# Layer 1's fronts in a two-layer mixer and expert kernel: both turned halves in one step, the row maximum a step behind the logits, scatters laid evenly and ended two steps ahead of the routed jobs

## The reference: what is computed

```python
x = L0_attn_x                                  # (4, 1024, 128)
xn = _layernorm(x)
s = _L0_attn_ref(xn, ...)   # a state-space scan over time, 256 channels x 16 states
g = _silu(_L0_ffn_ref(xn, ...))   # 8 experts, top 2, and a shared expert
x = x + s * g
xn = _layernorm(x)
s = _L1_attn_ref(xn, ...)   # linear attention, no softmax
g = _silu(_L1_ffn_ref(xn, ...))   # 8 experts of hidden size 176, top 2, and a gated shared one
x = x + s * g
```

## Time and profile before

| | |
|---|---|
| three runs | 1098.51, 1099.65, 1100.06 us; median 1099.65 us |
| the profiled execution, its own time | 1098.78 us |
| its span, first to last instruction | 1096.6 us |
| DVE busy | 940.8 us (86% of the span) |
| PE busy | 813.8 us (74%), mean granted clock 0.906 |
| POOL busy | 618.6 us (56%) |
| ACT busy | 577.2 us (53%) |
| scan of step 143, the last, begins | at 1028.97 us |
| from there to the end of the span | 67.6 us |

### The profile page before, as it was taken

One profiled execution on the slowest core, in us unless ns is written; L12 is line 12 of the kernel. 1 busy time (PEld: TensorE's weight loads), 2 busy tenths in 40 slices (PEclk: granted clock), 3 DMA queues, 4 the chain that ended last, 5 costly groups with the idle time before them and its releaser, 6 DMA issues.

```text
span 1096.6 us, 15959 instructions
## 1 busy us (share of the span) xinstructions
PE 813.8 (74%) x4378; PEld 595.6 (54%) x4378; DVE 940.8 (86%) x1608; ACT 577.2 (53%) x1296; POOL 618.6 (56%) x421
## 2 busy tenths in 40 slices
PE   7557576877877778768787678776686767678786
PEld 3444464565655656556665556564464645566564
DVE  5999989889988888999989979997979978879565
ACT  4446353665657455745566455645454535445333
POOL 1435885323678337534754776684885737623670
PEclk9778696999999989989999999998987889989998
DMA  8955954333444356435644447345753346446301
GB/s 250 266 162 151 250 145 129 111 90 90 128 120 140 94 140 168 129 80 141 171 109 119 128 139 183 95 146 152 180 140 79 101 112 185 112 93 137 99 27 34
DMA packets 169060, 146.07 MB, mean 133 GB/s; under 512 B 14433, under 2 KB 135825, under 8 KB 168977
## 3 DMA queue, kind: packets, MB, share of 16 engines
q10 hardware_dynamic: 38960, 66.00, 24.6%
q1 hardware_dynamic: 122337, 63.31, 20.2%
q0 software_dynamic: 7680, 15.74, 4.7%
HBM read 106.59 MB, written 37.88 MB: 132 GB/s over the span
## 4 chain that ended last, share of the span: by engine, by line
DVE 40%; PE 24%; issue 14%; POOL 7%; DMA 6%; ACT 6%; SPq 1%; ACTq 1%; DVEq 0%; POOLq 0%
DVE pA L1621 15%; DVE hj L1656 4%; POOL dBx L875 4%; PE pR L1125 3%; PE pGU L1084 3%; DVE hc L1629 3%; POOL rows_in L816 3%; PE pH L1010 3%; PE pGU L1081 3%; PE pGU L1082 3%; DMA xg<-rows_in 3%; DVE ca L1403 3%; DVE hj L1668 2%; ACT hT L1350 1%; DMA rows_in<-xn,slots 1%
## 5 line engine op out<-in xcount | busy, mean ns | idle before, releaser
L875 POOL TENSOR_TENSOR dBx<-dtx,bcb 128x1024 f32<-128x1024 f32 (+1 forms) x143 | 302.3, 2114 | 354.5 <-DVE pA L1621 323.0
L1010 PE MATMUL pH<-const,hc 128*128 128x128 f32 x1024 | 157.9, 301 | 100.7 <-DVE hc L1629 82.7
L1010 PEld LDWEIGHTS pH<-const,hc 128*128 128x128 f32 x1024 | 128.3, 155 | 122.8 <-DVE hc L1629 101.8
L1147 ACT ACTIVATE pA<-dt,am 128x512 f32<-128x512 f32 (+1 forms) x286 | 172.5, 637 | 27.9 <-DVE hc L1629 20.3
L1621 DVE TENSOR_TENSOR_SCAN pA<-pA,carry,dBx 128x512 f32<-128x512 f32 (+1 forms) x160 | 162.7, 1062 | 9.6 <-POOL dBx L875 5.5
L1629 DVE TENSOR_TENSOR hc<-pA,bcb 128x1024 f32<-128x1024 f32 (+1 forms) x144 | 159.3, 1106 | 5.0
L1621 DVE TENSOR_TENSOR_SCAN pA<-pA,dBx 128x512 f32<-128x512 f32 x128 | 149.7, 1215 | 4.5 <-ACT pA L1147 2.8
L1656 DVE SCALAR_TENSOR_TENSOR hj<-tj,pGU 128x352 f32<-128x352 f32 (+2 forms) x181 | 87.3, 482 | 59.0 <-ACT tj L1333 19.5
L834 POOL DMA_INDIRECT gy<-rows_out,slots x96 | 99.8, 1039 | 24.5 <-issue 19.9
L1099 PE MATMUL pR<-const,hj 128*88 128x128 f32 (+2 forms) x594 | 104.2, 291 | 9.4 <-issue 2.3
L1350 ACT ACTIVATE hT<-pR 128x384 f32<-128x384 f32 (+2 forms) x186 | 95.3, 512 | 13.9 <-PE pR L1099 12.5
(11 more groups left out here) (247 smaller groups left out, 1450.4 us busy)
## 6 DMA issues: line engine op xcount, KB each, us to landing
bcb<-bc_rows ACTq DMA_DIRECT2D x109, 512.0 KB, 5.0
xg<-rows_in SPq DMA_DIRECT2D x162, 64.0 KB, 2.8
bcb<-bc_rows ACTq DMA_DIRECT2D x32, 256.0 KB, 5.0
rows_out<-yj SPq DMA_DIRECT2D x114, 64.0 KB, 2.5
rows_out<-yj SPq DMA_DIRECT2D x54, 128.0 KB, 3.1
rows_in<-gy SPq DMA_DIRECT2D x12, 512.0 KB, 10.4
mixed<-s_st SPq DMA_DIRECT2D x12, 256.0 KB, 2.5
so<-rows_out SPq DMA_DIRECT2D x6, 512.0 KB, 4.7
```

The costliest lines, as they stand in the source:

```text
L875: pool.tensor_tensor(dBx[:, N % 2, :, 0:t1 - t0], dtx[q % 2][:, :, t0:t1], row, ALU.mult).then_inc(dBx_ready, 1)
L1010: last = mm(pH[:, half, c * DI + k * P:c * DI + (k + 1) * P], hc[:, N % 2, k, t * P:(t + 1) * P], ident, is_transpose=True, start=(n == 0 ...
L1147: A(pA[:, k, 0:t1 - t0], dt[q % 2][:, k, t0:t1], ACT.Exp, scale=am[:, k, n:n + 1]).then_inc(decay_ready, 1)
```

## The change

Only the table of `make_plan` changes; no instruction's shape does, and the computation stays the same.

```diff
-FFN3_AT, GATHER1_AT, GATHER2_AT = 107, 118, 139
+FFN3_AT, GATHER1_AT, GATHER2_AT = 107, 117, 135
...
-    FRONT = dict(first=1, norm=2, xn=3, xT=4, logits=6, top=7, route=8, pick=9, rank=10, slots=11, experts=14, scatter=12)
+    FRONT = dict(first=1, norm=2, xn=3, xT=4, logits=5, top=6, route=7, pick=8, rank=9, slots=10, experts=13, scatter=11)

-    def scatters(l, j, s, per_step):
+    def scatters(l, j, s, over):
         count = TOPK * cols(l, j)[1]
         for i in range(count):
-            at(s + i // per_step, "scatter", l, j, i)
-        return s + 1 + count // per_step
+            at(s + i * over // count, "scatter", l, j, i)
+        return s + over + (l == 1)
-
-    def front(b, s, per_step=3, **moved):
+    def front(b, s, over=5, **moved):
...
-            at(o["xT"] + 1, "xT", 1, b, 1)
+            at(o["xT"], "xT", 1, b, 1)
...
-        avail[1, b, "shared"] = o["xT"] + (2 if whole else 1)
-        avail[1, b, "routed"] = max(scatters(1, b, o["scatter"], per_step), o["experts"] + 1)
+        avail[1, b, "shared"] = o["xT"] + 1
+        avail[1, b, "routed"] = max(scatters(1, b, o["scatter"], over), o["experts"] + 1)
...
-    front(2, 96, 4, first=3, norm=3, xn=4, xT=6, logits=9, top=9, route=10, pick=11, rank=12, slots=13, experts=14, scatter=14)
+    front(2, 96, 4, first=3, norm=3, xn=4, xT=5, logits=6, top=7, route=8, pick=9, rank=10, slots=11, experts=13, scatter=12)
...
-    front(LAST, 7 * NS, 2, first=2, norm=2, xn=3, xT=5, logits=6, top=6, route=7, pick=8, rank=9, slots=10, experts=12, scatter=11)
-    front(LAST + 1, 8 * NS, first=1, norm=1, xn=2, xT=3, logits=4, top=4, route=5, pick=6)
+    front(LAST, 7 * NS, 3, first=2, norm=2, xn=3, xT=4, logits=5, top=6, route=7, pick=8, rank=9, slots=10, experts=12, scatter=11)
+    front(LAST + 1, 8 * NS, first=1, norm=1, xn=2, xT=3, logits=4, top=5, route=6, pick=6)
...
         for i in range(TOPK * CT):
-            at(s1 + i // (3 if b else 4), "gather", 1, b, i)
-        for part, step in zip(range(-1, 7), ((104, 106, 107, 108, 111, 113, 115, 116), (121, 124, 125, 126, 127, 129, 131, 132),
+            step = (s1 + i // 4, s1 + (i // 2 if i < 10 else 8 + (i - 10) // 3), s1 + i if s1 + i < STEPS else STEPS + 1)[b]
+            at(step, "gather", 1, b, i)
+        for part, step in zip(range(-1, 7), ((104, 106, 107, 108, 111, 113, 115, 116), (121, 127, 128, 129, 130, 132, 133, 134),
```

More of the change, by code:

```diff
@@ L187, in make_plan @@
         at(experts_at, "experts", 0, g)
-        avail[0, g, "routed"] = scatters(0, g, s + 5, 3)
+        avail[0, g, "routed"] = scatters(0, g, s + 5, 11)
     at(61, "x3T")
```

## The result

The changed kernel took **1115.8 us** (median of four executions, 1113.17 to 1128.33) against 1099.9 of the kernel before: a ratio of 1.015, 95% interval 1.0109 to 1.0191. It is slower; I had forecast 1095. In three of four later series of timings, each on another chip, the same kernel stood at 1.0018 (0.9991 to 1.0046), 1.0017 (0.9988 to 1.0047) and 1.0101 (1.0062 to 1.014) of before. So the loss lies between 1 and 16 us by the series: clear in the first comparison and the last, not to be told from zero in the two between, and a gain in none. The ratios leave out one execution of the kernel before that took 2178.8 us.

The account below looks back on a forecast made before the run. DVE, the busiest engine, was taken to bound the kernel, so terms counted idle time given back or taken; they summed to a gain of 4.5 us from the profiled 1098.78: 1094.3, or 1095 by the median. Range 1085 to 1102.

Parts of the forecast that it names:

- The fronts of batches 0 and 1: Steps 81 and 97: routed tiles a step earlier mostly move the waits; gain 1.8 and loss 1.0 us.
- The row maximum: Row maximum a step behind the logits: waits of 5.3 us in step 105 and 2.3 in step 132 go; gain 7.6.
- My rival of no change: Step 105's 5.3 us was ACT's queue, and the gate behind may wait for it instead: 1100 or 1098 us; chance 0.20.
- Batch 2, -0.55 net: Steps 108 to 115: wait of 6.2 us goes, POOL's load costs 5.7, gain 0.5; step 114's new gate loses 1.05.
- `dBx` as the releaser in steps 109 to 112: Sign that the forecast was right: DVE waits there for `dBx` on overloaded POOL, taken as 5.2 us over the stretch.
- Batch 1's fetch, -4.3: Steps 116 to 120: tiles behind the earlier fetch reach step 119's gate late; 30.8 against 26.47 us, loss 4.3.
- The wait at job 151's gate: Sign in step 119: 8 to 10 us if the forecast was right, under 4 if wrong.
- Way back of batch 1, -1.3: Steps 121 to 128: more indirect DMAs on POOL make DVE wait 9.7 to 11 us; loss 1.3.
- 22.4 to 24 us: Time from the start of step 123 until POOL issues the last gather of step 126.
- Gathers one a step, +3.9: Steps 135 to 142: batch 2's gathers one a step, 3.45 us a step, 27.6 + 0.3 against 31.79; gain 3.9.
- Behind the scans, -1.7: After the last scan's start: 15 gathers instead of 9 on POOL delay `combine`, one dense slot less; loss 1.7 us.

Follow-up runs that it names:

- second pair: Second profiles of the unaltered changed kernel (1106.69 us) and of the unaltered kernel before (1102.82 us), taken in two later series on two chips.
- second column: Stretch-by-stretch difference, changed kernel less kernel before, between the second profiles of each, from two later series on two chips: sum +4.7 us.

## Why the prediction was wrong, step by step

**The step that failed.** I added up idle gaps of DVE and gave each back, and put at nothing what the same entries do on POOL. Two terms show it. The fronts of batches 0 and 1, forecast as +0.8, alone made the kernel 3.7 us slower: steps 83 to 96, for which I had no term, took 5.5 more, in DVE instructions held by POOL. The row maximum was to give 5.3 in step 105 and gave 0.7. A third step had no term either: batch 2's fetch went from step 139 to 135, one step behind batch 1's store, and steps 135 to 142, forecast at -3.9, took 0.7 more (1.3 less in the second pair).

- **Row maximum, +7.6: failed in method.** In step 105 I gave the whole wait of 5.3 back and did not ask who is ready next. It was POOL, with 7.28 us a step and 0.75 idle; 0.7 came back. My rival of no change had this form, but named ACT. For the 2.3 of step 132, steps 129 to 134 were 1.1 shorter than in the first profile of before and 3.4 shorter than in the second.
- **Batches 0 and 1, +0.8: wrong by 5.5 us.** The gates of steps 81 and 97 waited 4.35 and 6.61, as worked out, and steps 64 to 82 gained 2.1. What I left out is steps 83 to 96. I had costed POOL's load in steps 108 to 112 and not in 91 to 95, where the same evenly laid scatters meet the same kind of addition (4.6 us in step 92), nor asked what POOL does during the wait that I moved out of step 82 (2.6 us in step 83). With the scatters back, both were gone.
- **Batch 2, -0.55 net: right that POOL is overloaded, wrong in the sign.** I had named `dBx` as the releaser in steps 109 to 112. DVE never waited for it there; it met the load as held instructions, 4.7 us of it in `cmp` and 1.3 to 1.4 in each of two operations on `w13a`. Steps 108 to 112 took 40.4 and 38.7 us for a forecast of 36.8; over 108 to 115 the size was off by 3.1 in the first profile and 1.7 in the second. The 3.35 us that I took for POOL's addition, here and behind the scans, was a held one; alone it takes 2.36.
- **Batch 1's fetch, -4.3: right.** 31.57 us for a forecast of 30.8; with the fetch moved back 27.4. Over all profiles it is 30.7 to 31.9 in six with the fetch in 117, and 26.0 to 28.2 in nine with it in 118, 30.0 in a tenth. The wait at job 151's gate was 4.4, not 8 to 10: the gate came 23.4 us into step 116 and not 25, and DVE had already waited 2.6 us in smaller pieces. What the term rests on is the measured way, 20.1 us from store to gate. That the tiles "cannot overtake" the fetch was more than the Trainium skill, "DMA: Bandwidth & Descriptors", section "Queues, rings and completion order", states: by it descriptors are taken in ring order, but DMAs need not complete in the order of their issue.
- **Way back of batch 1, -1.3:** taken with steps 129 to 134, I was off by 1.1 in the first profile. I had counted the two `combine` parts that leave steps 121 to 128, but not where they arrive. By my own figures the upper end of "22.4 to 24 us" should have been 25.4.
- **Gathers one a step, +3.9: right for the gathers.** They give 28.2 to 29.7 us in four profiles with the fetch three steps behind the store, and 3.5 us a step in steps 140 to 142, as forecast. It was wrong for the change, whose fetch stands one step behind: 30.3 to 32.5 in its four profiles. Which wait makes the difference is not shown, except for the kernel with the fetch in 133, where it is a gate's 6.29.
- **Behind the scans, -1.7.** 1.7 in the second pair, with DVE's `combine` waiting 5.63 for POOL as forecast; POOL's last gather was issued 32 us behind the last scan's start, not 34. Without the long row of gathers it was 63.0, so they cost 5.3, and the rest of the change there gained 3.6 to 4.6 against the two profiles of before. The 5.9 of the first profile hold the stall of PE.
- **The base.** The sum was made against one profile, and that one was 9.3 us shorter than the next profile of the same kernel, 4.4 of it before step 64 and 5.7 in steps 121 to 134.

Of the 16 us, those shown to belong to the change are steps 83 to 96 (5.5) and 116 to 120 (4 to 5), against which its gains stand. In the first and the third series the kernel's median is 3.0 and 1.0 us above before's, of the size of the second column's sum; the 16 and 10 us of the first comparison and the fourth series are not. What stays open is the rest of those two, and the stall of PE behind the scans, which is 7.8 and 9.3 us long in their profiles of this kernel. It takes part in the difference, but it also stands, at 3.4 us, in a profile of the kernel before, and what makes it is not known.

## What to carry to other kernels

Where an in-order engine waits, the gain from removing the wait is the distance to whoever is ready next; add up the other engines' queues for that step first, and for the step that the wait leaves. Read busy time as well as gaps: here a DVE instruction that took 5 us for 1 was always one held by POOL, and moving work on POOL moved such blocks. Keep a fetch that waits for a store several steps away from it when needed loads stand behind it in the queue, and take a second profile of the kernel before as the base.

## What the runs showed of the hardware

- DVE with two SBUF operands is held by POOL's tensor operations, through two in a row (4.6 us), and so are some instructions with one (`xn` 4.75 us for 2.13, `xs` 2.57 for 0.7). Indirect DMAs on POOL did not lengthen such an instruction (1.22 us in step 92 of the kernel with the additions moved), but were lengthened by it: the scatter beside it took 2.00 us, scatters beside the scans 0.95.
- Executions of one kernel spread over 0.8 to 1.7% (1096.8 to 1112.4 for before in the first series), and a longer time mostly goes with a lower mean granted clock (TensorE's, whose two levels are 1.2 and 2.4 GHz): for before in the fourth series 0.906 went with 1095.9 and 0.881 with 1109.4. Which follows from which is not shown.
- PE's records of `gram` ended 7.8 us ahead of ACT's copy, which waits for the semaphore of its last matmul (changed kernel, first profile). The granted clock was still 1.00 when this began and 0.50 from 1064.7 on, so the low clock came behind the stall and does not explain its start.
